# All even tiles of the probabilities in three rounded terms, the first seed from PSUM, and two more tiles summed by transfers

## What is computed

```python
# x (8, 56, 128), context (8, 1500, 128), mask (8, 56); heads 16, dim_head 64
k, v = jnp.split(context @ Wkv, 2, axis=-1)
q = _layernorm(x) @ Wq
q, k, v = (_split_heads(q), _split_heads(k), _split_heads(v))
dots = jnp.einsum('bhnd,bhmd->bhnm', q, k) * SCALE
dots = dots - (1.0 - mask.astype(jnp.float32))[:, None, :, None] * MASK_NEG
attn = jax.nn.softmax(dots, axis=-1)
out = jnp.einsum('bhnm,bhmd->bhnd', attn, v)
x = x + out.transpose(0, 2, 1, 3).reshape(b, n, h * d) @ Wout + bout
...
h = jax.nn.gelu(jnp.einsum('etd,edf->etf', tokens, w1) + b1[:, None, :])
y = jnp.einsum('etf,efd->etd', h, w2) + b2[:, None, :]
```

## Time and profile before

| | |
|---|---|
| three runs, us | 374.8, 375.22, 375.67 (median 375.22) |
| the profiled execution, us | 374.87 |
| its span in the profile, us | 373.0 |
| TensorE matmul busy, us | 363.0 |
| VectorE, ScalarE, POOL busy, us | 279.3, 255.1, 116.1 |

### The profile page before, as it was taken

One profiled execution on the slowest core, in us unless ns is written; L12 is line 12 of the kernel. 1 busy time (PEld: TensorE's weight loads), 2 busy tenths in 40 slices (PEclk: granted clock), 3 DMA queues, 4 the chain that ended last, 5 costly groups with the idle time before them and its releaser, 6 DMA issues.

```text
span 373.0 us, 5778 instructions
## 1 busy us (share of the span) xinstructions
PE 363.0 (97%) x1713; PEld 278.7 (75%) x1713; DVE 279.3 (75%) x458; ACT 255.1 (68%) x335; POOL 116.1 (31%) x125
## 2 busy tenths in 40 slices
PE   6899999999999999999999999999999999999996
PEld 6767777777777887777777877777777877687755
DVE  4888677978797669878797669878797669454863
ACT  3556576697769576697679476697579467796621
POOL 1610573245324430145324440255224440022000
PEclk9999999999999999999999999999999999999998
DMA  7686268329932854339932764349933752438400
GB/s 239 216 195 176 54 129 199 85 83 168 201 94 82 150 98 134 82 104 235 233 88 86 144 113 117 84 117 235 222 86 100 129 108 40 119 68 156 74 2 6
DMA packets 30622, 47.10 MB, mean 126 GB/s; under 512 B 2011, under 2 KB 21371, under 8 KB 30608
## 3 DMA queue, kind: packets, MB, share of 16 engines
q0 software_dynamic: 9936, 27.40, 37.6%
q1 hardware_dynamic: 20672, 19.52, 17.5%
HBM read 24.59 MB, written 0.23 MB: 67 GB/s over the span
## 4 chain that ended last, share of the span: by engine, by line
PE 85%; DVE 10%; issue 2%; ACT 1%; DMA 1%; SPq 0%; DVEq 0%; ACTq 0%
PE ps_s L444 29%; PE ps_a L484 23%; PE ps_x L500 10%; PE ps_a L477 9%; PE ps_x L533 3%; PE ps_a L421 2%; PE ps_x L553 2%; PE ps_x L458 1%; DVE shift_diag L930 1%; DVE ex_sum L900 1%; DMA ex_all<-in_wk_t 1%; PE ps_x L562 1%; DVE chunk_max L919 1%; DVE ex_lo L915 1%; PE ps_x L530 1%
## 5 line engine op out<-in xcount | busy, mean ns | idle before, releaser
L919 DVE TENSOR_REDUCE chunk_max<-ps_x 128x1 f32<-128x500 f32 x168 | 111.1, 677 | 31.9 <-PE ps_x L500 28.8
L708 ACT ACTIVATE ex_all<-ps_s 125x896 f32<-125x896 f32 x95 | 87.1, 917 | 44.1 <-PE ps_s L444 42.7
L484 PE MATMUL ps_a<-ex_all,ctx_sb 125*128 125x448 f32 x248 | 110.9, 541 | 0.0
L726 ACT COPY ps_s<-shift_row 125x896 f32<-125x896 f32 x94 | 85.7, 911 | 12.2 <-DVE shift_row L1057 9.7
L500 PE MATMUL ps_x<-ctxt_hi,qk_hi 128*128 128x500 f32 x168 | 80.7, 484 | 1.1 <-DVE chunk_max L919 0.9
L1234 POOL DMA_DIRECT2D ex_all<-ex_all x48 | 42.2, 878 | 115.9 <-ACT ex_all L708 111.6
L444 PE MATMUL ps_s<-qk_hi,ctxt_hi 128*125 128x448 f32 x192 | 76.3, 479 | 0.0
L484 PEld LDWEIGHTS ps_a<-ex_all,ctx_sb 125*128 125x128 f32 x248 | 46.3, 190 | 17.1 <-issue 12.7
L444 PE MATMUL ps_s<-qk_hi,ctxt_lo 128*125 128x448 f32 x192 | 54.9, 367 | 0.0
L444 PE MATMUL ps_s<-qk_lo,ctxt_hi 128*125 128x448 f32 x192 | 54.7, 366 | 0.0
L444 PEld LDWEIGHTS ps_s<-qk_hi,ctxt_hi 128*125 128x125 f32 x192 | 35.9, 187 | 24.4 <-issue 23.3
(11 more groups left out here) (110 smaller groups left out, 382.1 us busy)
## 6 DMA issues: line engine op xcount, KB each, us to landing
ex_all<-ex_all POOLq DMA_DIRECT2D x48, 448.0 KB, 4.6
ctxt_raw<-in_ctx_t SPq DMA_DIRECT2D x8, 750.0 KB, 6.5
ctx_sb<-in_ctx SPq DMA_DIRECT2D x8, 750.0 KB
ctxt_hi<-in_ctx_t POOLq DMA_DIRECT2D x21, 250.0 KB, 3.1
w_sb<-in_w SPq DMA_DIRECT2D x4, 512.0 KB, 5.0
w_sb<-in_w SPq DMA_DIRECT2D x8, 256.0 KB, 6.6
ex_all<-in_wq_t SPq DMA_DIRECT2D x2, 256.0 KB, 3.8
ex_all<-in_wk_t SPq DMA_DIRECT2D x2, 256.0 KB, 4.8
```

The costliest lines, as they stand in the source:

```text
L484: mm = nc.tensor.matmul(ps_a[:, c, 0:CH], ctx_sb[0:MT, u, t, :], ex(t)[0:MT, c * CH:(c + 1) * CH], start=(slot == 0), stop=(slot == TM - 1))
L708: nc.scalar.activation(half(ex(t)[0:MT, :]), src, ACT.Exp, scale=SCALE).then_inc(ex_ready, 1)
L726: nc.scalar.copy(ps_s[0:MT, t % 2, :, 0:CH], half(shift_row[0:MT, b.parity, :])).then_inc(seeded, 1)
L919: nc.vector.tensor_reduce(chunk_max[:, k, t:t + 1], filled()[:, 0:MC], AX.X, ALU.max).then_inc(job_free, 1)
```

## The change

Tiles 0 and 10 join the split tiles, so all six even tiles go in three terms (in the last batch tile 10 stays plain). The slots of tiles 10 and 11 are exchanged. Tiles 9 and 10 are added by transfers too, in chains [3, 6, 9], [4, 7], [5, 8, 10], and VectorE has three additions left, of tiles 1 and 11 and then 2; the last batch keeps its five. ScalarE makes the first seed of a batch straight from `ps_x`, and copies `shift_row` itself; the high part of tile 10 stands before that, the high part of the sums moves from step 0 to step 1. The score job of place (2, 2) moves to (9, 1). The context's high part has six tiles in place of four, and that of batch 0 is made before the later queries are drained. `sum_hi` takes the memory of `shift_diag`.

```diff
@@ -115,12 +115,13 @@
     HP = HEADS // 2
     TOK = 64
     CHAINS, RING, LAST_DMA = 3, 4, 8
-    SUM_PARTS = [9, 1, 10, 2, 11]
-    SUMS = len(SUM_PARTS)
-    SPLIT = [2, 4, 6, 8]
-    PV_ORDER = [0, 1, 2, 3, 5, 4, 7, 6, 9, 8, 10, 11]
+    CHAIN_TILES = [[3, 6, 9], [4, 7], [5, 8, 10]]
+    SUM_PARTS, LAST_SUM_PARTS = [1, 11, 2], [9, 1, 10, 2, 11]
+    SUMS, LAST_SUMS = len(SUM_PARTS), len(LAST_SUM_PARTS)
+    SPLIT = [0, 2, 4, 6, 8, 10]
+    PV_ORDER = [0, 1, 2, 3, 5, 4, 7, 6, 9, 8, 11, 10]
     SPLITS, CTX_HI_AT = len(SPLIT), 5
-    assert D == P and MT * TM == M and QT * P == Q and MC * KM == M and E == B and LAST_DMA % CHAINS == CHAINS - 1
+    assert D == P and MT * TM == M and QT * P == Q and MC * KM == M and E == B
@@ -131,11 +132,11 @@
     MAX_AT = [
-        [(1, 0), (1, 1), (1, 2), (2, 0), (2, 1), (2, 2), (4, 0), (4, 1), (4, 2), (5, 0), (5, 1), (5, 2),
...
+        [(1, 0), (1, 1), (1, 2), (2, 0), (2, 1), (4, 0), (4, 1), (4, 2), (5, 0), (5, 1), (5, 2),
+         (6, 0), (6, 1), (6, 2), (7, 0), (7, 1), (7, 2), (8, 0), (8, 2), (9, 0), (9, 1)],
...
@@ -143,8 +144,9 @@
     FOLD_AT = [(3, 0), (3, 2)]
     FIRST_SHIFT_AT, SHIFT_AT = (0, 1), (TM - 2, 2)
-    ADD_AT = {(10, 2): (0,), (11, 0): (1, 2)}
-    ADD_LATE = (3, 4)
+    ADD_AT = {(11, 1): (0,)}
+    ADD_LATE = {(0, 0): (1,), (0, 2): (2,)}
+    LOW_AT = [(t + 1, 1) for t in SPLIT[:-1]] + [(11, 0)]
     LAST_ADD_AT = {(10, 0): (0, 1), (11, 0): (2, 3)}
     GELU_AT = (9, 1)
     BEHIND = 2
@@ -183,7 +185,7 @@
         att = sb("att", [P, Q])
         log_sum = sb("log_sum", [P, Q])
         inv_sum = sb("inv_sum", [P, Q])
-        sum_hi = sb("sum_hi", [P, Q], F32R)
+        sum_hi = shift_diag[:, :, :].rearrange("p t q -> p (t q)")
         sum_lo = sb("sum_lo", [P, Q], F32R)
         att_n = sb("att_n", [P, HEADS, P])
@@ -276,14 +278,22 @@
             return PV_ORDER.index(t) + 1
+        def buffer_free(n):
+
+            return read_by(SPLIT[n - 2]) if n >= 2 else read_by(SPLIT[SPLITS - 2 + n]) - TM
+
+        def place_in_chain(t):
+
+            return next((c, tiles.index(t)) for c, tiles in enumerate(CHAIN_TILES) if t in tiles)
+
         def summed(t):
             return 1 + (SUM_PARTS.index(t) if t else 0)
         def added_by_dma(eng, b, t):
-            adds = LAST_DMA // CHAINS
-            eng.wait_ge(ex_added[t % CHAINS], b.at(16 * adds, 16 * (t // CHAINS)))
+            c, n = place_in_chain(t)
+            eng.wait_ge(ex_added[c], b.at(16 * len(CHAIN_TILES[c]), 16 * (n + 1)))
         def half(t):
@@ -475,7 +485,7 @@
                             between()
                         for c in range(2):
                             mm = nc.tensor.matmul(ps_a[:, c, 0:CH], a[0:MT, u, n, :], e[0:MT, n % 2, c * CH:(c + 1) * CH],
-                                                  start=False, stop=False)
+                                                  start=(slot == 0 and term == 0), stop=(slot == TM - 1 and term == 2))
                     mm.then_inc(pv_done, 1)
                     return
                 for c in range(2):
@@ -564,7 +574,8 @@
                 mm.then_inc(job_ready, 1)
             def shift_jobs():
-                for c in range(2):
+                for _ in range(2):
+                    c = jobs.n % 2
                     shift_rows(job()[:, 0:CH], P, c, start=True).then_inc(job_ready, 1)
             def iteration(b, prepare=True, pair=None):
@@ -711,8 +720,7 @@
                 t = SPLIT[n]
                 act.wait_ge(ex_ready, b.at(TM, t + 1))
-                if n >= 2:
-                    act.wait_ge(pv_done, b.at(TM, read_by(SPLIT[n - 2])))
+                wait(act, pv_done, b.at(TM, buffer_free(n)))
                 nc.scalar.copy(ex_hi[0:MT, n % 2, :], ex(t)[0:MT, :]).then_inc(ex_hi_ready, 1)
             def ctx_high_part(b):
@@ -724,6 +732,13 @@
                 act.wait_ge(ex_ready, b.at(TM, t - 1))
                 nc.scalar.copy(ps_s[0:MT, t % 2, :, 0:CH], half(shift_row[0:MT, b.parity, :])).then_inc(seeded, 1)
+
+            def first_seed(b):
+
+                act.wait_ge(job_ready, jobs.value())
+                act.wait_ge(ex_ready, b.at(TM, -1))
+                nc.scalar.copy(ps_s[0:MT, 0, :, 0:CH], ps_x[0:MT, :, 0:CH]).then_inc(seeded, 1)
+                nc.scalar.copy(half(shift_row[:, b.parity, :]), ps_x[:, :, 0:CH]).then_inc(job_free, 2)
             def att_out(b):
@@ -796,7 +811,10 @@
                             gelu_exp(pair)
                     exponentials(b, t)
                     if t == 1 and b.off > 0:
+                        sum_high_part(b.later(-1))
                         att_out(b.later(-1))
+                    if prepare and t == TM - 2:
+                        ex_high_part(b, SPLITS - 1)
                     if t + 2 < TM:
                         if t == 0 and first:
                             jobs.n += 2
@@ -805,15 +823,13 @@
                     elif prepare:
                         if t + 2 == TM:
                             jobs.n = FIRST_JOBS if first else jobs.n + 2
+                            first_seed(b.later(1))
+                        else:
                             act.wait_ge(job_free, jobs.value())
-                        seed(b.later(1), t + 2 - TM)
-                    if t == 0 and b.off > 0:
-                        sum_high_part(b.later(-1))
-                    if t == 1 and first:
-                        ctx_high_part(b)
+                            seed(b.later(1), 1)
                     if t == CTX_HI_AT and prepare:
                         ctx_high_part(b.later(1))
-                    if t in SPLIT:
+                    if t in SPLIT[:-1]:
                         ex_high_part(b, SPLIT.index(t))
                     if pair is not None and t == GELU_AT[0]:
                         gelu_sigmoid(pair)
@@ -846,6 +862,7 @@
             drain_fold(3)
             drain_queries(2)
             drain_queries(3)
+            ctx_high_part(Batch(None, 0))
             for h in range(HEADS):
                 drain_later_queries(h)
             jobs.n = 2 + QT * KM
@@ -887,21 +904,20 @@
             def add_to_sum(b, n):
-                t = SUM_PARTS[n]
+                parts, by_dma = (LAST_SUM_PARTS, LAST_DMA) if b.off == B - 1 else (SUM_PARTS, TM)
+                t = parts[n]
                 dst = ex_sum[0:MT, b.parity, :]
                 left = ex(0)[0:MT, :] if n == 0 else dst
-                if n == 0:
-                    added_by_dma(dve, b, LAST_DMA - CHAINS + 1)
-                if t < CHAINS:
-                    added_by_dma(dve, b, LAST_DMA - CHAINS + 1 + t)
-                else:
+                for c in ((0,) if n == 0 else ()) + ((t,) if t < CHAINS else ()):
+                    added_by_dma(dve, b, max(s for s in CHAIN_TILES[c] if s <= by_dma))
+                if t >= CHAINS:
                     dve.wait_ge(ex_ready, b.at(TM, t + 1))
                 wait(dve, ex_summed, b.at(SUMS, n))
                 nc.vector.tensor_tensor(dst, left, ex(t)[0:MT, :], ALU.add).then_inc(ex_summed, 1)
             def add_last(b):
-                dve.wait_ge(ex_summed, b.at(SUMS, SUMS - 1))
+                dve.wait_ge(ex_summed, b.at(SUMS, LAST_SUMS - 1))
                 for c in range(2):
                     cols = slice(c * CH, (c + 1) * CH)
                     dve.wait_ge(ex_ready, b.at(TM, TM + c))
@@ -1052,8 +1068,8 @@
             def shift_copies(b):
-                wait(dve, seeded, b.at(TM, -TM - 2))
-                for c in range(2):
+                for _ in range(2):
+                    c = jobs.n % 2
                     nc.vector.tensor_copy(shift_row[:, b.parity, c * CH:(c + 1) * CH], filled()[:, 0:CH]).then_inc(job_free, 1)
             def sum_low_part(b):
@@ -1067,7 +1083,7 @@
                     if b.off == 0 and at == FIRST_SHIFT_AT:
                         shift_copies(b)
                     if prepare and at == SHIFT_AT:
-                        shift_copies(b.later(1))
+                        jobs.n += 2
                     if b.off == 0 and at in FOLD_AT:
                         for r in range(2):
                             folded(2 * FOLD_AT.index(at) + r)
@@ -1107,13 +1123,12 @@
                         add_last(b)
                 def add(at):
-                    if at == (0, 0) and b.off > 0:
-                        for n in ADD_LATE:
-                            add_to_sum(b.later(-1), n)
+                    for n in ADD_LATE.get(at, ()) if b.off > 0 else ():
+                        add_to_sum(b.later(-1), n)
                     for n in (ADD_AT if prepare else LAST_ADD_AT).get(at, ()):
                         add_to_sum(b, n)
-                    if (at[0] - 1, at[1]) in [(t, 1) for t in SPLIT]:
-                        ex_low_part(b, SPLIT.index(at[0] - 1))
+                    if at in LOW_AT and (prepare or LOW_AT.index(at) < SPLITS - 1):
+                        ex_low_part(b, LOW_AT.index(at))
                 for t in range(TM):
                     drain((t, 0))
@@ -1226,12 +1241,13 @@
```

(13 more changed lines are left out.)

10 lines of the change are left out of this document (4 added, 6 removed), and 5 rows, old and new, of the table MAX_AT.

## The result

The changed kernel takes **392.16 us** (median of four runs, 390.89 to 393.54) against 375.01 before (374.57 to 375.67, four runs): the ratio is 1.0457, 95% interval 1.0412 to 1.0501. The prediction, 379.3 with a range of 375.4 to 381.0, had the direction and missed the size by 13 us. The profiled execution of the changed kernel took 391.39, with a span of 389.2 us; before it was 374.87 and 373.0. So 16.2 us of span are to be found.

What follows compares the result with a forecast made beforehand. TensorE, busy 97% of the span, was taken as the bound. 374.87 - 4.2 (work gone) + 2.8 (shift row) + 1.1 (batch 0) + 0.5 (last batch) + 3.1 (start) + 1.1 (clock) = 379.3 us, range 375.4 to 381.0.

Steps and rivals of the forecast that it cites:

- The start: Before the first scores: ScalarE's early cast waits for the context load, landing at about 20.0, delaying later queries: +3.1 us.
- What goes: TensorE work saved by turning 15 tiles from plain fp32 into three terms, 0.28 us each: 4.2 us less.
- VectorE was seldom what TensorE waited for: At the additions and shift-row copies taken off VectorE: the reason to credit nothing for that relief.
- The shift row: At each batch boundary the moved job makes shift_diag late, TensorE waiting about 0.4 us longer, seven times: +2.8 us.
- the 0.24 us said to be waiting already: Around the shift matmuls between tile 9's halves: 0.24 us of existing TensorE wait, read as no slack there.
- Batch 0: At step 2 of batch 0, tile 0's low part among VectorE's maxima makes TensorE's job (2, 1) wait: +1.1 us.
- The last batch: Without score jobs ScalarE sets the pace, and TensorE waits for its copy of ps_a: +0.5 us.
- The clock: After TensorE's 3 us idle gap at the start, the granted clock falls: +1.1 us (0 to 1.7).
- The whole 1.7: The clock loss at the start counted in full, by the Trainium skill's rule: 1.7 us, sum 379.9.
- Transfers late: Rival at batch boundaries: accumulating transfers of tiles 9 and 10 land late, 1 us a batch, 386; over 382 given 0.07.

Runs made afterwards that it cites:

- C4: Changed kernel, cast behind drains, ctxt_raw loaded later, maximum back at (2, 2), POOL's query parts earlier, VectorE's low part of the sums behind maximum (2, 0): 373.37 us, 0.9963.
- E5: Changed kernel with the row maximum moved back from place (9, 1) to (2, 2): 388.57 us, ratio 1.0342.
- E3: Changed kernel with the 750 KB load of ctxt_raw held until ctxt_hi of the same batch has landed: 384.07 us, ratio 1.0229.
- E4: Changed kernel with POOL's low parts of queries and first ctxt chunk waiting for VectorE's low part of tile 2: 393.60 us, ratio 1.0506.
- E8: Changed kernel with accumulating chains 1 and 2 swapped, so tile 10's transfer goes behind tile 7's, not tile 8's: 385.59 us, ratio 1.0277.

## Why the prediction was wrong

Two steps failed. The start was mis-sized, in its landing and in its clock: 3.1 and 1.1 in the sum, 5.3 and 2.5 measured. And the transfers at the batch boundary were put at nothing, since one landing was compared with the cover where two stand in a chain: they cost 5.3. A third loss, VectorE beside POOL, 2.2, had no term at all.

- **What goes, 4.2: right.** In the changed kernel steps 2 and 3 are 0.83 to 0.87 shorter, 0.2 of it the job that moved away. That leaves 0.6 a batch, the 2 x 0.28 forecast; in C4, with most of the stalls gone, TensorE is busy 358.2 us against 363.0 before. What I did not see is that this holds only while the job is elsewhere: with it at (2, 2) VectorE is the bound there. "VectorE was seldom what TensorE waited for" was read from the kernel with the slower tiles.
- **The shift row, 2.8: right**, 0.36 to 0.45 a batch without its job, and E5 takes most of it away. One reading behind it was not: the 0.24 us said to be waiting already without a pair is no wait in the trace (the three waits before are those with a pair) but for the most part the price behind a plain tile that the last section shows.
- **Batch 0, 1.1: right.** TensorE's job (2, 1) stands at 44.82 with 0.78 of waiting, and the piece is 1.17 longer; 0.4 for the shift row and 0.28 less for tile 0 leave 1.05 of that.
- **The last batch, 0.5: right.** Its piece is only 0.1 shorter, with two tiles' gain of 0.56 in it (tile 10 of the batch before, and its own tile 0). In the changed kernel ScalarE's copy of `ps_a` ends 6.7 us behind the start of scores(0) at 334.00, where 6.9 was forecast, and TensorE's next product into `ps_a` comes 0.93 behind the pair of scores ahead of it, in place of 0.4. The profile names no releaser for it, but it starts 0.21 behind the copy's end. Timeline:
```profile
339.80 0.91 ACT L747 COPY att<-ps_a 128x896 f32<-128x896 f32 x1
340.92 0.65 PE L487 MATMUL ps_a<-ex_hi,ctx_hi 125*128 125x448 f32 x2 [0.37 <-issue]
```
- **The start, 3.1: the step that failed was the landing.** I read it from the end of the short packets in the earlier trace rows. They do end there, but in the same trace the last semaphore update of this load is at 21.43, 1.4 us later, and a wait ends with that: in the nine profiled runs with the early cast, the cast starts within 0.03 us of it, at 21.1 to 22.3. The changed kernel's was the latest of them, at 22.3. The block is 5.3.
- **The clock, 1.1: direction right, size 2.5.** I took the price from gaps far shorter and let part of the slow stretch lie in the gap. A part did, 1.1 us, but 5.7 us of it lay behind the gap. The rule of the Trainium skill that stands beside this term in the prediction (TensorE: Matmul & The Clock Gate, "What's actually happening") agrees in kind, an idle TensorE falls back. The whole 1.7 would have been too small as well.
- **Transfers late: given a chance of 0.07, and it happened, on two paths at once.** I compared the median landing of 4.6 with some 6 us of cover for VectorE's last addition. But tile 10's transfer waits for tile 8's, which was slow before the change already. From the end of exp(10) at 197.25 to that addition at 205.85 it was 8.6 us, so 2.6 more than the cover; 2.1 were paid there. I said that a context load runs among these transfers (it is `ctxt_raw`, 750 KB), and still took the median. The second path I did not see: the loads of `ctxt_hi` go out right behind tile 10's transfer, and TensorE waits for them. Together they cost 1.3 to 2.1 us in each of three batches, 5.3 in all by the profile, and E3 takes away all of it. How much either path would cost alone no run shows.
- **Not in the prediction at all:** VectorE slowed beside POOL, 0.75 in each batch with a pair. In the kernel before, POOL's subtraction at this place ended at 200.08 and the low part of tile 2 started at 200.09.

In the prediction's own terms: 379.3, plus 2.2 and 1.4 at the start, plus 5.3 for the boundaries and 2.2 for step 4, is 390.4; the profiled execution took 391.39. Most of what is left stands in batches 1, 3 and 5, which by the sum would be 0.5 shorter than before in all and are 0.6 longer.

## What to carry to other kernels

When a transfer is added to a queue, follow what it waits for itself, and what goes out behind it: here it waited for a slow landing, and was then in flight beside the next batch's loads. Ask which large load moves in that window. A median landing over the whole run hides the collision, and a slow transfer for which nobody waits costs nothing until a change puts a wait on it. Taking away the collision gave all of the loss at step 1 back, shortening the wait 3.0 of 5.3. The last packet of a load is not its landing. An instruction that waits for a load may go early only if nothing stands behind it that the busiest engine wants, and time saved on that engine is kept only where the engine that drains it has room.

## What the runs showed of the hardware

- Where a VectorE operation on two SBUF operands and a POOL subtraction overlapped, the one that started second took up to 0.9 us longer: so in all 75 overlaps of 0.3 us and more between VectorE's operations on 896 columns and POOL's in these traces. In the changed kernel VectorE starts second (213.67 behind 213.41) and takes 1.94 in place of 1.09, in E4 the refinement 1.98. In E8 it starts first, and POOL's subtraction takes 2.13 in place of 1.25; this is the 1.8 of its step 4. Maxima and products that read PSUM kept their 0.68 and 0.62 beside POOL (E4). The Trainium skill (SBUF — State Buffer, "Who interferes with whom") has these operations take their second operand by a path shared with GpSimd, and reductions never contend; these runs agree. Timeline of E8:
```profile
210.00 1.09 DVE L931 TENSOR_TENSOR ex_lo<-ex_all,ex_hi 125x896 fp32r<-125x896 f32 x1 [1.19 <-ACT ex_hi L724]
210.07 2.13 POOL L1239 TENSOR_TENSOR ctxt_lo<-ctxt_raw,ctxt_hi 128x500 fp32r<-128x500 f32 x1
```
- After 5.4 us without work TensorE ran at 1.2 GHz for another 5.7 us, 2.53 us of loss; with useless matmuls in that gap the clock stayed at 2.4 GHz and the same work took 10.38 us, as before.
- The price of a plain fp32 tile is partly paid behind it. In C4 the first two products after a plain tile take 0.75 us to the next pair (201.31 to 202.06), after a tile in three terms 0.41 (198.10 to 198.51), so the gain of a tile shows in the step after its own:
```profile
198.10 0.57 PE L454 MATMUL ps_s<-qk_hi,ctxt_hi 128*125 128x448 f32 x2
198.51 0.57 PE L454 MATMUL ps_s<-qk_lo,ctxt_hi 128*125 128x448 f32 x2
201.31 0.92 PE L454 MATMUL ps_s<-qk_hi,ctxt_hi 128*125 128x448 f32 x2
202.06 0.57 PE L454 MATMUL ps_s<-qk_lo,ctxt_hi 128*125 128x448 f32 x2
```
